# A binary 3x3 convolution: thirteen sets of four images interleaved value by value, in tiles of four rows in place of pairs in tiles of seven

## What is computed

```python
def _gn(v, G=32, eps=1e-5):              # group norm, 8 channels a group
    ...
    return ((g - m) / jnp.sqrt(s + eps)).reshape(v.shape)

A = m * m + jnp.sum(z * z, axis=0) / SCALE      # m, z: M and the 8 Z's, flat
inv = lax.rsqrt(A)
w = (rv @ (z * inv))[0] + m * inv
bw = jnp.sign(w).reshape(256, 256, 3, 3)
ba = jnp.sign(_gn(x))
out = x + alpha * conv(ba, bw)           # 3x3, stride 1, padding 1
```

## Time and profile before

| what | value |
|---|---|
| median of 3 runs | 480.31 us (479.12 to 480.69) |
| the profiled execution's own time | 480.06 us |
| span of the profiled execution | 478.3 us, so 1.8 us lie around the span |
| PE busy | 451.8 us (94%), 2966 matmuls, of them 2304 convolution |
| PE weight loads busy | 424.5 us (89%) |
| DVE busy | 397.0 us (83%) |
| ACT busy | 326.1 us (68%) |
| DMA | 124.55 MB, 260 GB/s on average |
| mean granted PE clock | 0.985 |

### The profile page before, as it was taken

How to read it: one execution, slowest core, us unless ns; L and a number is a source line. 1 busy time by engine, 2 the same in 40 slices (tenths; PEclk the granted TensorE clock), 3 DMA queues, 4 the chain that set the end, 5 groups by cost and what they waited for, 6 DMA issues and landing times.

```text
span 478.3 us, 8267 instructions
## 1 busy us (share of the span) xinstructions
PE 451.8 (94%) x2966; PEld 424.5 (89%) x2966; DVE 397.0 (83%) x781; ACT 326.1 (68%) x564; POOL 10.8 (2%) x55
## 2 busy tenths in 40 slices
PE   3778898999999999999999999999999999999994
PEld 1333467999999999999999999999999999999994
DVE  2468687899989898989898989899898989898686
ACT  2556887785959494949494959586777768594420
POOL 3000000000000000000000000000000000000000
PEclk9979999999999999999999999999999999999998
DMA  7999999078777777777776776767766677632345
GB/s 268 399 394 391 392 356 393 13 259 325 259 259 253 252 268 271 269 271 269 264 274 222 270 263 253 252 235 275 257 259 254 250 252 252 250 120 117 134 182 223
DMA packets 46234, 124.55 MB, mean 260 GB/s; under 512 B 3696, under 2 KB 4208, under 8 KB 46192
## 3 DMA queue, kind: packets, MB, share of 16 engines
q1 hardware_dynamic: 45488, 123.21, 70.4%
q10 hardware_dynamic: 704, 0.81, 0.5%
HBM read 72.62 MB, written 51.38 MB: 259 GB/s over the span
## 4 chain that ended last, share of the span: by engine, by line
PE 80%; ACT 5%; SPq 4%; DVE 4%; DMA 3%; issue 2%; DVEq 0%; ACTq 0%
PE conv_ps L402 76%; SPq L283 4%; DMA x_sb<-in_L_conv_Z_dram 2%; ACT signs L550 2%; PE wt_ps L360 2%; PE conv_ps L340 1%; DVE low L856 1%; DVE whole L847 1%; DMA part<-in_L_conv_M_dram 1%; DVE x_sb L875 1%; ACT unread L531 1%; ACT unread L533 1%; ACT whole L498 1%; SPq L286 1%; PE conv_ps L347 1%
## 5 line engine op out<-in xcount | busy, mean ns | idle before, releaser
L402 PE MATMUL conv_ps<-signs,wts 128*128 128x378 f32 (+3 forms) x2304 | 403.9, 337 | 3.1 <-ACT part L564 2.2
L402 PEld LDWEIGHTS conv_ps<-signs,wts 128*128 128x128 f32 x2304 | 401.1, 189 | 6.3 <-ACT part L564 3.3
L550 ACT ACTIVATE signs<-x_sb,shift,rstd 128x784 fp32r<-128x784 f32 x128 | 133.7, 1099 | 21.3 <-DVE shift L833 21.3
L564 ACT ACTIVATE part<-conv_ps 128x392 int32<-128x392 f32 x128 | 62.4, 487 | 68.3 <-PE conv_ps L402 68.3
L847 DVE SCALAR_TENSOR_TENSOR whole<-conv_ps,part 128x392 int32<-128x392 f32 x128 | 72.2, 564 | 38.5 <-PE conv_ps L402 34.9
L856 DVE SCALAR_TENSOR_TENSOR low<-whole,conv_ps 128x392 f32<-128x392 int16 x128 | 71.9, 562 | 4.4
L777 DVE BATCH_NORM_STATS2 bn<-x_sb 128x6 f32<-128x392 f32 x138 | 70.6, 556 | 0.0
L875 DVE SCALAR_TENSOR_TENSOR x_sb<-whole,alpha_sb,x_sb 128x1568 f32<-128x1568 int16 (+1 forms) x38 | 60.6, 1594 | 0.8
L875 DVE SCALAR_TENSOR_TENSOR x_sb<-low,alpha_sb,x_sb 128x1568 f32<-128x1568 f32 (+1 forms) x38 | 60.4, 1588 | 0.0
L533 ACT ACTIVATE unread<-x_sb 128x784 bf16<-128x784 f32 x59 | 50.4, 854 | 0.0
L531 ACT ACTIVATE unread<-x_sb 128x784 bf16<-128x784 f32 x59 | 50.2, 851 | 0.0
(11 more groups left out here) (56 smaller groups left out, 118.1 us busy)
## 6 DMA issues: line engine op xcount, KB each, us to landing
x_sb<-in_x_dram SPq DMA_DIRECT2D x64, 784.0 KB, 5.0
out_dram<-x_sb SPq DMA_DIRECT2D x62, 784.0 KB, 4.8
x_sb<-in_L_conv_Z_dram SPq DMA_DIRECT2D x64, 288.0 KB, 9.0
part<-in_L_conv_M_dram SPq DMA_DIRECT2D x8, 288.0 KB, 10.1
out_dram<-x_sb SPq DMA_DIRECT2D x1, 588.0 KB, 3.9
out_dram<-x_sb ACTq DMA_DIRECT2D x1, 588.0 KB, 4.5
out_dram<-x_sb SPq DMA_DIRECT2D x2, 98.0 KB, 3.2
out_dram<-x_sb ACTq DMA_DIRECT2D x2, 98.0 KB, 3.5
```

The costliest lines, as they stand in the source:

```text
L402: mm = pe.matmul(flat_tile(conv_ps[at][:, 0:COLUMNS], b, r0, r1, c0, c1), wts[:, ch, (down + 1) * KW + right + 1], e, start=n == 0, stop=n ...
L550: nc.scalar.activation(o, x_sb[:, slot_of(k * TRI + image), h], ACT.Sign, bias=shift[:, k % RING, image, h:h + 1], scale=rstd[:, k % RING, ...
L564: nc.scalar.activation(part[:, at, 0:COLUMNS], conv_ps[at][:, 0:COLUMNS], ACT.Copy, scale=-FRACTION / PACK, bias=FRACTION / 2).then_inc(pa ...
```

## The change

The sets 2 to 14 (thirteen) are no longer split into pairs. Their four images lie interleaved value by value in one array: a row is 112 numbers, the values of one image lie 16 bytes apart, and a tile is four rows, 448 columns, so a set has seven tiles. A tap that shifts sideways has 432 columns in four pieces. All sizes now hang on the set number k (`paired(k)`). The outputs of such a set come in two parts, rows 0 to 11 (three tiles) and rows 12 to 27, each for all four images (`output_fours`), the stores likewise (336 KB and 448 KB an image), and the four loads follow the second part together. The next set's half images are in another order: the first half of all four, then the second. `signs` changes the order of its dimensions from pair, half to half, pair. The sets 0, 1 and 15 keep their pairs, but their order changes: image 2's first half goes from ACT to DVE (ALONE has a 2 more), ACT takes the third tile's fraction ahead of `deviation` and of the four signs of the second pair, DVE makes `group_steps(1)` before the statistics of image 4, and in set 1 the `group_steps` of set 2 come before the sums of its second to fourth tile. The diff, cut to its core:

```diff
+FOUR_ROWS = 4
+TOP_PART = 12
...
+    FOURS = H // FOUR_ROWS
...
-        signs = sb("signs", [P, 2, PAIRS, HALVES, SPAN], F32R)
+        signs = sb("signs", [P, 2, HALVES, PAIRS, SPAN], F32R)
...
-        ALONE = (0, 1, 4, 5, 9)
+        ALONE = (0, 1, 2, 4, 5, 9)
...
+        def paired(k):
+            return k < 2 or k == LAST_SET
+        def tiles_of(k):
+            return TILES if paired(k) else FOURS
...
+        def row_span(k, b):
+            return (b % TOPS * TOP_ROWS, (b % TOPS + 1) * TOP_ROWS) if paired(k) else (b * FOUR_ROWS, (b + 1) * FOUR_ROWS)
+        def row_of(k):
+            return ROW if paired(k) else ROW * PAIRS
+        def columns(k):
+            return TOP_ROWS * ROW if paired(k) else FOUR_ROWS * ROW * PAIRS
...
-            for q in range(LAST_SET * PAIRS):
-                sp.wait_ge(out_done, (q + 1) * HALVES)
-                for j in range(PAIR):
-                    store_rows(q * PAIR + j, 0, H)
-                for j in range(PAIR):
-                    if q * PAIR + j + SLOTS < N:
-                        load(q * PAIR + j + SLOTS)
+            for k in range(LAST_SET):
+                for q in range(PAIRS):
+                    sp.wait_ge(out_done, (k * PAIRS + q + 1) * HALVES)
+                    if paired(k):
...
+                    else:
+                        for j in range(TRI):
+                            store_rows(k * TRI + j, q * TOP_PART, TOP_PART if q == 0 else H)
+                if not paired(k):
+                    for j in range(TRI):
+                        if k * TRI + j + SLOTS < N:
+                            load(k * TRI + j + SLOTS)
...
             def half_signs(g, k, n):
+                if paired(k):
...
+                else:
+                    h, image = divmod(n, TRI)
+                    o = signs[:, k % 2, h].rearrange("p q f -> p (q f)").rearrange("p (f i) -> p i f", i=TRI)[:, image]
...
+            def output_fours(k, h, r0, r1):
+                slot = slot_of(k * TRI)
+                dve.wait_ge(low_done, first_tile(k) + r1 // FOUR_ROWS)
+                v = (whole if h == 1 else low)[:, k % 2].rearrange("p q f -> p (q f)")[:, r0 * ROW * PAIRS:r1 * ROW * PAIRS]
+                v = (high(v) if h == 1 else v).rearrange("p (f i) -> p i f", i=TRI)
+                o = x_sb[:, slot:slot + TRI, h, r0 * W:r1 * W]
+                nc.vector.scalar_tensor_tensor(out=o, in0=v, scalar=alpha_sb[:, h:h + 1], in1=o, op0=ALU.mult,
+                                               op1=ALU.add).then_inc(out_done, 1)
```

More of the change, by code:

```diff
@@ L291, in load @@
                 if i >= SLOTS:
-                    sp.wait_ge(stored[slot_of(i)], i // SLOTS * 16)
+                    sp.wait_ge(stored[slot_of(i)], 16 * sum(stores(n) for n in range(slot_of(i), i, SLOTS)))
                 sp.dma_start(x_sb[:, slot_of(i)], x_v[i]).then_inc(x_loaded[slot_of(i)], 16)
@@ L326, in _ @@
             for n in range(SLOTS):
-                parts = 1 + HALVES if n in (slot_of(N - 2), slot_of(N - 1)) else 1
-                sp.wait_ge(stored[n], 16 * (len(range(n, N, SLOTS)) - 1 + parts))
+                sp.wait_ge(stored[n], 16 * sum(stores(i) for i in range(n, N, SLOTS)))
         @block.tensor
@@ new lines, in _ @@
+            set_signs(1, 6, 8)
+            fraction(1, 1)
+            sums(2 * TRI + 2)
+            fraction(1, 2)
+            sums(2 * TRI + 3)
+            fraction(1, 3)
+            deviation(turn(2), 2, 0, TRI)
+            set_signs(2, 0, 2)
+            fraction(1, 4)
+            set_signs(2, 2, 5)
+            fraction(1, 5)
+            set_signs(2, 5, 7)
+            fraction(1, 6)
+            set_signs(2, 7, 8)
+            sums(3 * TRI)
+            fraction(1, 7)
+            sums(3 * TRI + 1)
@@ new lines, in _ @@
+            group_steps(turn(2), 2, 3 * TRI)
+            tile_sums(1, 0)
+            bounded(turn(2), 2, 0, TRI)
+            negative_mean(turn(2), 2, 0, TRI)
+            for b in range(1, TOPS):
+                tile_sums(1, b)
+            output(1, 0, 1, TOPS)
+            output(1, 0, 0, TOPS)
+            image_stats(3 * TRI, lambda: tile_sums(1, 4))
+            image_stats(3 * TRI + 1, lambda: tile_sums(1, 5))
+            for k in range(2, LAST_SET):
+                g = turn(k + 1)
+                image_stats((k + 1) * TRI + 2, lambda: tile_sums(k - 1, tiles_of(k - 1) - 2))
+                tile_sums(k - 1, tiles_of(k - 1) - 1)
+                second_outputs(k - 1)
```

209 lines of the change are left out of this document (105 added, 104 removed).

## The result

The changed kernel takes **537.2 us** (535.34 to 538.21), the kernel before in the same session 480.34 (479.12 to 480.69): a ratio of 1.119, with a 95% interval of 1.117 to 1.121. The forecast was 472.4 us, its range ended at 500.0. The profiled execution has a span of 533.6 us against 478.3, 55.3 us more.

The account below looks back on a forecast made before the run. The prediction took PE's convolution to bound the kernel. It took 4.9 us from the middle sets and 3.0 us from the first sets, 7.9 us together, off 480.31 us: 472.4 us, range 467.5 to 500.

Parts of the forecast that it names:

- What bounds the kernel: Middle sets before the change: PE is the limit, 25.00 us a set, and DVE has 2.9 us to spare.
- Change 3: DVE's sums and outputs in the middle sets: 16-byte reads cost nothing extra, DVE fits with 21.8 us in 24.6.
- the first rival: DVE's outputs in the middle sets: slower 16-byte reads make DVE the bound, 26.1 us a set, 492 us; chance 0.28.
- Change 4: ACT's fractions and signs in the middle sets: at most 2.0 us more a set, which fits; effect nil.
- a full second cycle: DVE's outputs at 1.04 ns more per value: 28.3 us a set, 520 us in all.
- Change 2: PE's sideways matmuls in the middle sets: fewer, longer pieces gain 0.38 us a set, 4.9 us with the fixed part included.
- The upper end: PE's cut pieces in the middle sets: no left-out column is lost any more, 24.33 us a set.
- The middle case: PE's cut pieces in the middle sets: each loses two columns whatever its length, 24.62 us a set; the one taken.
- Change 1: PE's matmuls in the middle sets, 126 for 144: a fixed part of 5.1 ns each gives 0.09 us a set.
- Change 5: Stores in two parts and four bunched loads on SP's queue: the loads land in time, effect nil.
- The spare: Bunched loads behind the second outputs: some 3 us in hand, 1 us a set for each us beyond.
- Change 6: New order of the first two sets: PE's 1.84 us gap and slow clock go, 3.0 us gained, between nothing and 4.0.

Follow-up runs that it names:

- run 5: Changed kernel, middle sets' signs written 4, 8 and 12 bytes apart, outputs read 12 and 24 bytes apart (not the reference's output): 503.31 us.
- run 11: Changed kernel with the next set's group steps ahead of the second outputs, and outputs cut at row 16 in place of 12: 514.67 us.
- run 2: Changed kernel, but ACT writes the middle sets' signs 8 bytes apart as before (not the reference's output): 510.65 us.
- run 4: Kernel before, pairs kept in all sets, with only the change's new order of the first sets: 480.73 us, ratio 1.0018.
- run 8: Changed kernel in another layout: seven tiles, each with two pairs side by side, no 16-byte step, reference output kept: 480.69 us, ratio 1.0015.
- run 3: Changed kernel, middle sets' outputs read and signs written 8 bytes apart (not the reference's output): 472.74 us, ratio 0.9848.
- run 7: Changed kernel, order only: next set's last statistics and group steps ahead of the second outputs, ACT's signs earlier: 536.36 us, ratio 1.1169.

## Why the prediction was wrong

- **What bounds the kernel**: right for before. The yardstick of 25.00 us a set served in every run.
- **Change 3 failed.** It put the price of the 16-byte step in DVE's reads at nothing: "I take nothing, since the only widening of the step that rows show was free". The step costs 1.86 - 1.04 = 0.82 ns a value, above the 0.45 ns from which the first rival decides and above its 0.68. At 8 bytes two values still share 16 bytes, and at 16 they no longer do, which fits the prices of run 5; to carry the free step on was the mistake. Both rules of the Trainium skill named under the first rival spoke against it, and that rival got 0.28 against 0.58.
- **Change 4 failed too, and it wasn't among the rivals.** Its surcharge was to be 245 ns a sign if the price of the 8-byte step doubled; it is 680 ns (1780 against 1099). "Nil" rested on eight signs and four fractions fitting into 14 us behind `deviation`: with the measured 1780 and 558 ns they want 14.2 + 2.2 = 16.4. In the trace the signs with two of the fractions take 13.7 us, in a circle that had no spare.
- **The first rival had the right mechanism and too small a time**: 26.1 us a set and 492 us. DVE's real need is 26.4 to 26.7 us; with this alone in the way (27.6 a set as in run 11) it is 515 us. The other 22 us are mostly the circle of the signs (some 29.3 us a set instead of 27.6), which no rival had: DVE and ACT stand one behind the other between two sets, so that what both lose adds up. Even the 520 us for a full second cycle lay below the 537. Most of set 1's 5.6 us belongs here as well: with the signs 8 bytes apart (run 2) it takes 26.0 us, with them 16 apart 30.6. The other 1.0 to 1.5 us are there without any 16-byte step (26.5 us in run 4), so they go with the new order of the first sets.
- **Change 2 was undersized.** The upper end, "nothing is lost any more", is what PE does: 24.42 us a set, 0.58 less, 7.5 us over thirteen sets. The middle case was taken for want of a row.
- **Change 1** took 0.09 us a set too much: run 8 shows no fixed part. The 5.1 ns were a remainder of two close numbers.
- **Change 5** held in the changed kernel and in run 3: no wait for a load. The spare was real but small; run 7, which ended the second outputs later, fell through it and lost what it had gained.
- **Change 6 failed**: 3.0 us forecast, 0.15 measured in run 4. The idle slices of DVE were added up as if they lay where the work had moved; between 78 and 90 us DVE was already full, and the gap moved to 91 us.
- That the kernel would take 472 us if the byte steps were free came out by luck: run 3 has 472.74, but by 7.5 us from PE and none from the first sets, in place of 4.9 and 3.0.

## What to carry to other kernels

When a layout widens the distance between neighbouring values, price every engine that reads or writes it, and measure the very step that the change uses: a step that was free says nothing about the next. Where two engines work one behind the other between two stages, follow the way round once and add up, since two engines busy for 91% and 79% of the time can still make a circle without any spare. And an order that breaks one circle by moving an output later must be followed to the load that waits behind it.
